# Feed-forward: queries and keys turned by 64x128 blocks in two row halves of TensorE's array

## The reference, cut to what matters

```
h = shift_token(x)
q, k, v = split(h @ wqkv)                    # 8 heads of 64
q, k = l2norm(q) * qs, l2norm(k) * ksc
q, k = rotary_xpos(q, k)
o = local_attention(q, k, v)                 # windows of 64, each sees itself and the one before
x = x + o @ wo
h = layernorm(shift_token(x)) * lg + lb
a, g = split(h @ w1 + b1)
x = x + (a * gelu(g)) @ w2 + b2
```

## Time and profile before

| | |
|---|---|
| median of 3 runs | 2494.72 us (2492.01 to 2496.49) |
| the profiled execution's own time | 2494.18 us |
| its span, first to last instruction | 2492.4 us |
| TensorE busy | 2238.0 us, 90% of the span |
| VectorE, ScalarE, GpSimd busy | 69%, 59%, 44% |
| mean granted TensorE clock | 0.952 |

### The profile page before, as it was taken

The page is one execution under the profiler, slowest core; times in us unless marked ns, Lnnn a source line. Parts: engine busy times, 40 slices in busy tenths (PEclk is TensorE's granted clock), DMA queues, the critical chain, the costliest instruction groups (busy, mean ns, idle before and its releaser), DMA issues. The chain is left out here.

```text
span 2492.4 us, 52712 instructions
## 1 busy us (share of the span) xinstructions
PE 2238.0 (90%) x21606; PEld 1670.2 (67%) x21606; DVE 1709.9 (69%) x2815; ACT 1465.2 (59%) x2389; POOL 1095.6 (44%) x800
## 2 busy tenths in 40 slices
PE   1799999999999969999969999999999997597968
PEld 1577777777777646666646777777777775495758
DVE  3677777778888636777737777777788784563556
ACT  0476767666676515555546677766676664363635
POOL 4655555656555210000025565656555560550245
PEclk8799999999999969999989999999999998698979
DMA  7000000069999970000000000000000002221022
GB/s 152 1 1 1 2 1 1 1 76 119 131 147 147 147 85 1 2 2 2 2 1 1 2 1 1 1 2 2 1 2 1 1 1 68 55 70 38 33 74 81
DMA packets 211362, 90.88 MB, mean 36 GB/s; under 512 B 79700, under 2 KB 206721, under 8 KB 210996
## 3 DMA queue, kind: packets, MB, share of 16 engines
q1 hardware_dynamic: 202596, 72.27, 21.8%
q0 software_dynamic: 6080, 11.76, 1.5%
q10 hardware_dynamic: 2448, 3.48, 0.7%
HBM read 24.51 MB, written 63.41 MB: 35 GB/s over the span
## 5 line engine op out<-in xcount | busy, mean ns | idle before, releaser
L477 POOL TENSOR_TENSOR work<-work,rot_tables 128x512 f32<-128x512 f32 x256 | 446.5, 1764 | 440.7 <-ACT work L581 440.7
L485 POOL TENSOR_TENSOR work<-work 128x1024 f32<-128x1024 f32 x128 | 305.2, 2384 | 13.0 <-DVE work L911 3.1
L911 DVE TENSOR_TENSOR work<-work,rot_tables 128x1024 f32<-128x1024 f32 x128 | 162.2, 1268 | 112.2 <-ACT work L581 112.2
L1068 DVE TENSOR_REDUCE small<-psum 128x4 f32<-128x1024 f32 x128 | 156.5, 1223 | 95.5 <-PE psum L1584 95.4
L1310 PE MATMUL psum<-qkv_w_hi,h_hi 128*128 128x512 f32 x384 | 182.7, 476 | 18.9 <-POOL h_lo L504 16.4
L1464 PE MATMUL psum<-centered,ffn_w 128*128 128x256 f32 x768 | 190.3, 399 | 6.1 <-DVE centered L972 2.9
L928 DVE TENSOR_TENSOR work<-work,small 128x1024 f32<-128x1024 f32 x128 | 159.5, 1248 | 51.2 <-ACT small L595 47.0
L692 ACT ACTIVATE work<-psum 128x1024 f32<-128x1024 f32 x128 | 131.2, 1025 | 102.2 <-PE psum L1591 102.2
L1402 PE MATMUL psum<-work 64*128 64x128 f32 (+1 forms) x2048 | 180.8, 307 | 0.0
L492 POOL TENSOR_TENSOR y_all<-centered,squared 64x256 f32<-64x256 f32 x64 | 48.7, 761 | 295.0 <-ACT squared L641 292.4
L1464 PEld LDWEIGHTS psum<-centered,ffn_w 128*128 128x128 f32 x768 | 145.8, 196 | 36.2 <-DVE centered L972 17.7
(11 more groups left out here) (285 smaller groups left out, 5718.6 us busy)
## 6 DMA issues: line engine op xcount, KB each, us to landing
h_area<-mean_weights SPq DMA_DIRECT2D x24, 2048.0 KB
tile_x<-h_area SPq DMA_DIRECT2D x39, 128.5 KB, 2.1
stage<-in_consts ACTq DMA_DIRECT2D x1, 3009.0 KB, 12.6
tile_x<-h_area SPq DMA_DIRECT2D x39, 64.5 KB, 1.8
work<-in_x SPq DMA_DIRECT2D x4, 512.0 KB, 27.4
expert_w<-in_ew SPq DMA_DIRECT2D x1, 2048.0 KB, 8.6
expert_w<-in_ew SPq DMA_DIRECT2D x8, 256.0 KB, 6.9
work<-y_tokens SPq DMA_DIRECT2D x4, 512.0 KB, 6.1
```

The costliest lines, as they stand in the source:

```text
L477: last = pool.tensor_tensor(b[:, :, :, o_], a[:, :, :, i_], tab[:, l, 1, t, :, o_].unsqueeze(2).to_broadcast([P, 2, HEADS, 32]), ALU.mult)
L485: pool.tensor_tensor(rC[:, t, :], rC[:, t, :], rB[:, t, :], ALU.add).then_inc(f_sum, 1)
L911: dve.tensor_tensor(g(rC[:, t, :]), g(rA[:, t, :]), tab[:, l, 0, t, :, :].unsqueeze(2).to_broadcast([P, 2, HEADS, DH]), ALU.mult)\
L1068: dve.tensor_reduce(dst, PS[:, 0:2, :].rearrange("p b (t j) -> p b t j", t=TILES), AX, ALU.max, negate=True).then_inc(a_smax, 1)
```

## The change

The 128x128 transpose becomes two of 64 partitions by 128 columns, each against the 64x64 corner of the identity that lies in its own partitions, each into a bank of its own: the upper 64 tokens of a tile into bank b0, the lower 64 into b0 + 1. So a bank holds 8 blocks of 64 tokens (4 chunks c, 2 tiles t) where it held 2 chunks of 256 tokens. The copies out of PSUM put the tokens back in order by their access pattern (`by_half`, `in_halves`); kT, qT and their bf16 copies are laid out as before. Waits and increments stand where they stood.

```diff
+        def by_half(banks):
+            return banks.rearrange("p b (n x) -> p b n x", x=64)
+
+        def in_halves(a):
+            return a.rearrange("p c (t b x) -> p b (c t) x", t=TILES, b=2)
...
                 def copy_q(i):
                     act.wait_ge(f_qT, i + 1)
-                    q = PS[:, 3:5, :]
-                    act.activation(qT.rearrange("p (b c) t -> p b (c t)", b=2), q, ACT.Copy)
-                    act.activation(qb[:, :, :].rearrange("p (b c) t -> p b (c t)", b=2), q, ACT.Copy).then_inc(f_qsb, 1)
+                    q = by_half(PS[:, 3:5, :])
+                    act.activation(in_halves(qT), q, ACT.Copy)
+                    act.activation(in_halves(qb[:, :, :]), q, ACT.Copy).then_inc(f_qsb, 1)
...
                 def k_out(i):
                     dve.wait_ge(f_kT, i + 1)
-                    link(dve.tensor_copy(kT.rearrange("p (b c) t -> p b (c t)", b=2), PS[:, 5:7, :]))
+                    link(dve.tensor_copy(in_halves(kT), by_half(PS[:, 5:7, :])))
                     dve.tensor_copy(kb[:, :, :], kT).then_inc(f_kb, 1)
...
+            def turned(b0, t, at_):
+                for c in range(4):
+                    for r in range(2):
+                        k_ = slice(64 * r, 64 * r + 64)
+                        o = (2 * c + t) * 64
+                        last = pe.transpose(PS[:, b0 + r, o:o + 64], rC[k_, t, at_ + c * P:at_ + (c + 1) * P], eye[k_, k_])
+                return last
+
                 def qk_T(i):
                     free(pe, f_p, 3 * i - 1)
                     for t in range(TILES):
                         pe.wait_ge(f_nrm, 2 * i + t + 1)
-                        for c in range(4):
-                            o = (c % 2) * T + t * P
-                            last = pe.transpose(PS[:, 5 + c // 2, o:o + P], rC[:, t, INNER + c * P:INNER + (c + 1) * P],
-                                                eye[:, :])
+                        last = turned(5, t, INNER)
                         if t == TILES - 1:
                             last.then_inc(f_kT, 1)
                         else:
                             free(pe, f_on, 2 * i - 1)
-                        for c in range(4):
-                            o = (c % 2) * T + t * P
-                            last = pe.transpose(PS[:, 3 + c // 2, o:o + P], rC[:, t, c * P:(c + 1) * P], eye[:, :])
+                        last = turned(3, t, 0)
                     last.then_inc(f_qT, 1)
```

## The result

| | before | after |
|---|---|---|
| median of 10 runs each, same chip | 2495.12 us (2491.88 to 2498.46, and one of 2851.13) | 2472.32 us (2468.26 to 2485.15) |
| ratio | | 0.9923, 95% interval 0.9911 to 0.9935 |
| profiled execution, its span | 2494.18, 2492.4 us | 2473.8, 2471.8 us |

The ratio and its interval leave out the one run of 2851.13 us, which is 14% above the others; they are not the quotient of the two medians, which is 0.9909. So the gain is 0.8 to 0.9%. The forecast was 2473.2 us, in a range of 2467 to 2491. In the rows of the kernel after L609 stands for L601 of before, L589 for L581, L1377 for L1366, L1382 for L1371 and L1464 for L1453.

The account below looks back on a forecast made before the run. It took TensorE, 90% busy, as first suspect, with the transposes on the path in layer 1 but beside the `h_lo` chain in layer 0. Saving 21.4 - 0.35 = 21.0 us from 2494.18 gave 2473.2 us, range 2467 to 2491.

Parts of the forecast that it names:

- Pace of a pair: Two half transposes running at once take 0.060 us against 0.109 for a whole one; 436 pairs save 21.4 us.
- Layer 0 gives nothing: In 30 turns of layer 0 the projection waits for GpSimd's `h_lo`, so a shorter turning saves nothing.
- Layer 1: 27 turns with 12 pairs, 7 with 16: Turns where the saving counts: 12 pairs behind the `o_norm` wait in 27, all 16 in 7; 436 pairs together.
- Exit from row tiles: Change from row tiles to the whole array before the projection: at most 0.09 us per item, put at 0.
- The way into row tiles: Change into row tiles before the transposes: 0.05 us extra, counting 7 times, 0.35 us in all.
- Copies at 0: Copies out of PSUM in runs of 64, same number of elements: no change in time.
- First items at nothing: The first item of each block, at the lower clock, saves nothing.
- A: Rival: saving partly there, a pair taking 0.07 to 0.10 us, or slower copies or exit; 2477 to 2490 us; chance 0.12.
- D: Rival: the halves run one after the other, up to 0.218 us a pair; 2592 us; chance 0.08.
- B: Rival: weight loads set the pace, 0.114 us a pair, so no gain; 2496 to 2500 us; chance 0.09.
- C: Rival: layer 0 gains as well, its GpSimd chain moved by earlier copies; 23 us more, 2450 us; chance 0.05.

Follow-up runs that it names:

- x_var_mid: Kernel after, with the matmul `x_var` moved one group earlier, between the two product groups of the first attention half: 2458.75 us, ratio 0.9852 to the kernel before.
- before_x_var_mid: Kernel before (whole transposes), with `x_var` moved between the two product groups of the first attention half: 2494.23 us, ratio 0.9977.
- upper_half_only: Kernel after, with both transposes of each pair reading the upper 64 partitions, so none runs in the lower half: 2508.18 us, ratio 1.0051 to the kernel before.
- twice_layer_1: Kernel after, with every group of transposes in layer 1 done twice: 2519.96 us, ratio 1.0101 to before; with the `h_area` transfer moved behind block 1, 2506.41 us.
- halves_layer_1: Kernel after, with half transposes in layer 1 only and whole transposes with their copies in layer 0: 2481.04 us, ratio 0.9943 to the kernel before.
- keys_first: Kernel after, with both tiles' keys transposed before the `o_norm` wait and both tiles' queries behind it: 2472.58 us, ratio 0.9909 to the kernel before.
- twice_layer_0: Kernel after, with every group of transposes in layer 0 done twice: 2478.01 us, ratio 0.9929 to the kernel before.
- one_half_then_other: Kernel after, with the transpose loops exchanged: four blocks of the upper half, then four of the lower: 2479.06 us, ratio 0.9941 to the kernel before.

## Why the prediction was right, point by point

- *Pace of a pair, taken as 0.060 (bounds 0.057 and 0.112).* 0.063 by the loads (the row of 24 in 0.83 us). A term of 0.046 us a pair instead of 0.049; over 436 pairs 20.1 us instead of 21.4. The reason given (the loads' spacing of 0.06) fits: alone in one half they come every 0.062. The reading that 64 columns of f32 stream in 0.055 was not separated from it.
- *Layer 0 gives nothing.* Right: 24.83 against 24.85, the `h_lo` wait 0.76 us longer against 0.8. x_var_mid shows the cause by taking it away. The statement that 0.43 us were to spare there holds for the projection alone: through ScalarE's copies the turning had only 0.11 us to spare, as before_x_var_mid and upper_half_only show.
- *Layer 1: 27 turns with 12 pairs, 7 with 16.* Right: the 32 turns between items of layer 1 gave 18.9 us; 26 of them were 0.55 us shorter in the median, and six, which wait for no `o_norm` before or after (those of items 15, 16 and 17 of each block), were 0.74: 23.80 before, 23.06 after. 26 x 0.55 + 6 x 0.74 = 18.7. The seventh of the prediction, item 20 of block 1, recorded no wait before but has one after. The last item of each block, which the forecast's 34 also holds, lies in the stretches behind the blocks and can't be told apart there: the forecast's 21.0 less 1.3 for the pace and 2 x 0.55 for these two is 18.6.
- *Exit from row tiles, at most 0.09 us, put at 0 under a thin cover.* The sum was right, the bound was not, and the cover works by another way than the scores. Counted from the start of the turning, the projection comes 1.90 - 1.51 = 0.39 us sooner, while 12 pairs are worth 0.55: 0.16 us go to the change of shape and what comes with it, more than the bound. The masks (L1377) start 0.25 us behind ScalarE's `copy_qk`, where the earlier trace rows have 0.15, and so come only 5.18 - 4.72 = 0.46 sooner: TensorE itself now ends that wait. L1464 comes 7.11 - 6.56 = 0.55 sooner again, since its distance behind the scores was 0.76 us before and is 0.66 now. In the kernel before it had waited for VectorE's `y_all`, which comes behind `copy_qk`:

```profile
729.08 0.73 PE L1371 MATMUL psum<-kT_bf,qT_bf 64*128 64x128 bf16 x16
729.84 0.70 PE L1453 MATMUL psum<-y_all,mean_weights 128*128 128x256 f32 x2
```

  The turn itself follows `copy_qk`, which ends 5.03 us after the start of the turning before and 4.47 after. The copies wait for the last transpose and not for the projection behind it, and so the exit costs nothing as long as TensorE's own work stays within the gaps that its waits for them leave. It has now all but filled them. The way into row tiles, put at 0.35 us in all, can't be told apart from the rest.
- *Copies at 0.* Right: 1026, 1017, 1225 ns.
- *First items at nothing.* They came out 4.3 us shorter, but not by the change: twice_layer_1 and its version with the transfer moved have the same program there, and 29.6 and 29.5 us against 25.5 and 27.2. The clock granted in this stretch differs. Here are 96 to 102 us, the kernel before, then after:

```profile
96.00:102.00 6.00, 2.95 (x11) 1.59 (x10) 5.93 (x7) 2.36 (x3) 4.43 (x4) 0.77 0.00 0
```
```profile
96.00:102.00 6.00, 5.36 (x48) 3.87 (x48) 5.90 (x10) 3.00 (x3) 4.89 (x4) 1.00 0.00 0
```

  That these 4.3 us and the 1.3 ahead of the first turning nearly cancel the 4.2 in attention and the end is chance. The turns alone gave 19.0 us of the 21.0 forecast, so a forecast within 0.9 us of the median, and 0.6 of the profiled execution, is closer than its terms were.
- *Rivals.* A (0.07 to 0.10 a pair) and D (one after the other) fall with the pace, D also because upper_half_only shows what no concurrency costs: 24.16 us a turn. B falls too: a half takes its 128 columns of weights every 0.062 us. By the Trainium skill, "TensorE: Matmul & The Clock Gate", LDWEIGHTS (columns / 1.2 ns), it would be 0.107, an estimate; the measurement decides. C falls with the unchanged turn of layer 0; its saving is there once x_var_mid starts the chain to `h_lo` earlier.

My own weak step was in the experiments: I held the order of the program for the order of the array, and it is not, between the two halves.

## What to carry to other kernels

A transpose of f32 that fills the array can be cut into two row halves for about 0.58 of its time (here with a PSUM bank for each half; a shared one wasn't tried); count the gain only in turns where TensorE or what follows the transposes ends the wait, and look for the next chain behind the one that does. If a chain of other engines ends it, start that chain earlier first: here moving one pair of products by one group, with the halves, was worth 0.57 us a turn, where the two alone gave 0.12 and 0.02. To find where chains meet, look for one instruction whose end, taken from the turn, leaves the same rest in every version; here it was a copy on ScalarE. Compare medians of one repeated turn, and treat the total of a single profile as the noisier number.

## What the runs showed of the hardware that I had not expected

- The halves of the array start 0.013 us apart (as the spacing of the loads tells) even where four transposes of the one half stand ahead of the other's in the program, and the turn is 0.05 us longer, not 0.55.
- A half transpose alone in its half takes 0.062 us, against 0.109 for a whole one of twice the columns of output and the same 128 columns of weights.
- Twice the transposes in layer 1 brought no stall until a large transfer ran beside them: then single waits of 1 to 3.3 us without a releaser appeared, and behind the longest of them 6 us at a granted clock of 0.50. The kernel after, with 8 packets more on the instruction queue than before (181 against 173), shows none in its feed-forward; halves_layer_1 and x_var_mid show 5 us in block 1, keys_first and twice_layer_0 2 to 3, upper_half_only and one_half_then_other 1.
